# Feed-forward: the gated chunk computed twice from the PSUM bank, once rounded and once in full, in place of a rounding copy

## What is computed

```python
h = silu(x @ w1.T * w1_s) * (x @ w2.T * w2_s)     # 128 -> 512
h = gelu(h @ h1.T * h1_s)                          # 512 -> 512
h = gelu(h @ h2.T * h2_s)                          # 512 -> 512
return h @ w3.T * w3_s                             # 512 -> 128
```

## Time and profile before

| | us |
|---|---|
| median of 3 runs | 766.37 |
| lowest and highest run | 765.67, 766.99 |
| the profiled execution's own time | 768.21 |
| span of the profiled execution | 766.4 |
| TensorE (PE) matmuls busy in the span | 685.7 (89%) |
| VectorE (DVE) busy | 484.8 (63%) |
| ScalarE (ACT) busy | 454.9 (59%) |
| GpSimd (POOL) busy | 431.0 (56%) |
| mean granted TensorE clock | 0.977 of full speed |

### The profile page before, as it was taken

One profiled execution on the slowest core, in us unless ns is written; L12 is line 12 of the kernel. 1 busy time (PEld: TensorE's weight loads), 2 busy tenths in 40 slices (PEclk: granted clock), 3 DMA queues, 4 the chain that ended last, 5 costly groups with the idle time before them and its releaser, 6 DMA issues.

```text
span 766.4 us, 13977 instructions
## 1 busy us (share of the span) xinstructions
PE 685.7 (89%) x4706; PEld 472.0 (62%) x4706; DVE 484.8 (63%) x957; ACT 454.9 (59%) x801; POOL 431.0 (56%) x444
## 2 busy tenths in 40 slices
PE   3789896799999999999999999999878899999996
PEld 1455555477787777665555555555445777777784
DVE  6668885567555586456767767766658356675510
ACT  2677774555665565445656566666665555556663
POOL 4455441377867776433444544543555677777763
PEclk9999998899999999999999999999999999999998
DMA  6110320000000003531645654645111000000000
GB/s 182 39 38 20 62 27 2 0 1 1 0 1 0 0 0 99 177 111 43 209 147 177 239 169 156 229 140 180 57 63 41 16 15 15 14 0 15 15 15 27
DMA packets 33028, 52.47 MB, mean 68 GB/s; under 512 B 4560, under 2 KB 9680, under 8 KB 32976
## 3 DMA queue, kind: packets, MB, share of 16 engines
q1 hardware_dynamic: 32784, 51.53, 21.3%
q10 hardware_dynamic: 192, 0.26, 0.1%
HBM read 27.15 MB, written 24.38 MB: 67 GB/s over the span
## 4 chain that ended last, share of the span: by engine, by line
PE 48%; DVE 13%; POOL 13%; issue 12%; ACT 8%; DMA 5%; ACTq 1%; POOLq 1%; DVEq 0%; SPq 0%
PE banks L220 44%; POOL f_h_lo L1122 5%; POOL f_g_lo L1129 5%; ACT b_prob L1448 2%; DMA b_o_dram<-b_o 2%; DVE xn L182 2%; DVE a_mx L645 2%; PE banks L212 2%; ACT a_prob L548 1%; DMA b_den<-b_o_dram 1%; DVE a_prob L657 1%; DVE f_hidden L1072 1%; DVE a_straight L630 1%; PE banks L957 1%; DVE f_gate L1068 1%
## 5 line engine op out<-in xcount | busy, mean ns | idle before, releaser
L1129 POOL TENSOR_TENSOR f_g_lo<-f_gelu,f_g_hi 128x512 fp32r<-128x512 f32 x128 | 167.9, 1316 | 68.8 <-ACT f_g_hi L1024 68.5
L1023 ACT ACTIVATE f_gelu<-banks,cols 128x512 f32<-128x512 f32 x128 | 88.2, 689 | 141.9 <-PE banks L220 139.3
L220 PE MATMUL banks<-f_g_hi,whi 128*128 128x512 f32 x320 | 132.7, 415 | 15.1 <-POOL f_g_lo L1129 15.1
L1534 DVE TENSOR_REDUCE b_segment_max<-banks 128x6 f32<-128x768 f32 x128 | 116.2, 949 | 45.0 <-PE banks L220 44.6
L1644 POOL TENSOR_SCALAR_AFFINE_SELECT b_prob<-b_prob 128x512 f32<-128x512 f32 x128 | 81.7, 641 | 111.6 <-ACT b_prob L1448 111.4
L1448 ACT ACTIVATE b_prob<-banks 128x768 f32<-128x768 f32 x128 | 102.6, 809 | 63.4 <-PE banks L220 55.0
L220 PE MATMUL banks<-f_g_lo,whi 128*128 128x512 f32 x320 | 128.1, 400 | 0.0
L1122 POOL TENSOR_TENSOR f_h_lo<-f_hidden,f_h_hi 128x512 fp32r<-128x512 f32 x60 | 77.5, 1292 | 58.7 <-DVE f_h_hi L1075 58.7
L220 PE MATMUL banks<-f_h_hi,whi 128*128 128x512 f32 x256 | 104.4, 408 | 3.2 <-POOL f_h_lo L1122 2.7
L220 PE MATMUL banks<-f_h_lo,whi 128*128 128x512 f32 x256 | 102.1, 399 | 0.0
L1024 ACT ACTIVATE f_g_hi<-banks,cols 128x512 fp32r<-128x512 f32 x128 | 87.1, 680 | 0.0
(11 more groups left out here) (124 smaller groups left out, 1052.1 us busy)
## 6 DMA issues: line engine op xcount, KB each, us to landing
f_h_hi<-b_q_dram SPq DMA_DIRECT2D x16, 512.0 KB, 4.0
f_h_lo<-b_k_dram SPq DMA_DIRECT2D x16, 512.0 KB, 5.0
b_o_dram<-b_o SPq DMA_DIRECT2D x8, 1024.0 KB, 4.3
b_q_dram<-b_q_hi SPq DMA_DIRECT2D x16, 256.0 KB, 3.2
b_k_dram<-b_k_hi SPq DMA_DIRECT2D x16, 256.0 KB, 3.3
w_stage<-in_wF SPq DMA_DIRECT2D x8, 352.0 KB, 3.2
b_q_dram<-b_q_lo SPq DMA_DIRECT2D x8, 256.0 KB, 3.4
b_k_dram<-b_k_lo SPq DMA_DIRECT2D x8, 256.0 KB, 3.8
```

The source lines that it names most:

```text
L220: return nc.tensor.matmul(out, lhsT, rhs, start=start, stop=stop)
L1023: nc.scalar.activation(gf[c % 2][:, :], z_bank[c % 2], ACT.Gelu, scale=scale).then_inc(s_gf, 1)
L1129: nc.gpsimd.tensor_tensor(lo[:, c, :], gf[c % 2][:, :], hi[:, c, :].bitcast(F32), ALU.subtract).then_inc(s_glo[c % 2], 1)
L1534: nc.vector.reduce_max(seg[:, g, s, 2 * p:2 * p + 2, :], first_pass[:, 2 * p:2 * p + 2, 0:3 * P].rearrange("p b (c k) -> p b c k", c=3), A ...
```

## The change

In `dve_gate` the copy L1075 goes. In its place the instruction of L1072 is made twice: first with `f_h_hi` as its output, so that the rounding happens at its write, then with `f_hidden` as before. The wait for the buffer of `f_hidden` now stands between the two. Each subtraction waits for both. The order of the rest is unchanged.

```diff
                 dve.wait_ge(s_u, KC * t + c + 1)
+                nc.vector.scalar_tensor_tensor(out=hhi[n.odd][:, c, :], in0=b[:, :], scalar=sc[:, 1, c:c + 1],
+                                               in1=uu[slot][:, :], op0=ALU.mult, op1=ALU.mult).then_inc(s_hhi, 1)
                 dve.wait_ge(s_hlo[slot], 2 * t + c // 2)
                 nc.vector.scalar_tensor_tensor(out=hf[slot][:, :], in0=b[:, :], scalar=sc[:, 1, c:c + 1],
                                                in1=uu[slot][:, :], op0=ALU.mult, op1=ALU.mult).then_inc(s_hf[slot], 1)
-                dve.wait_ge(s_hf[slot], 2 * t + c // 2 + 1)
-                nc.vector.tensor_copy(hhi[n.odd][:, c, :], hf[slot][:, :]).then_inc(s_hhi, 1)
 
             def dve_hlo(dve, n, c):
                 dve.wait_ge(s_hhi, KC * n.t + c + 1)
+                dve.wait_ge(s_hf[c % 2], 2 * n.t + c // 2 + 1)
                 nc.vector.tensor_tensor(hlo[n.odd][:, c, :], hf[c % 2][:, :], hhi[n.odd][:, c, :].bitcast(F32),
                                         ALU.subtract).then_inc(s_hlo[c % 2], 1)
...
             def pool_hlo(pool, n, c):
                 pool.wait_ge(s_hhi, KC * n.t + c + 1)
+                pool.wait_ge(s_hf[c % 2], 2 * n.t + c // 2 + 1)
                 nc.gpsimd.tensor_tensor(hlo[n.odd][:, c, :], hf[c % 2][:, :], hhi[n.odd][:, c, :].bitcast(F32),
                                         ALU.subtract).then_inc(s_hlo[c % 2], 1)
```

## The result

The changed kernel takes 760.35 us in the median of four runs (760.00 to 763.38), the kernel before 766.43 beside it; the ratio is 0.993, with a 95% interval from 0.9903 to 0.9957. A second set of six runs gave 761.15 us against 767.21, ratio 0.9908 (0.9874 to 0.9943).

A forecast was written before the change was run, and what follows sets the result against it. The prediction took a feed-forward block's length to be set by the loop through gate products, VectorE's gate work and copy, and POOL's subtractions, for which TensorE waits. Its terms summed to -2.6 us, giving 763.8 us, range 761.8 to 766.7.

The forecast's parts named there:

- seams of feed-forward 1: Later VectorE work with nothing to hide it: +0.55 us in the head, +0.4 in block 6 of feed-forward 1.
- block 5: In both feed-forwards, POOL's idle times behind the hindered copies go: -0.6 us, of which -0.4 stays in feed-forward 1.
- block 0 of feed-forward 2: Copies of 1.52 and 1.49 us go; with VectorE's later work, the block ends 0.4 us sooner.
- steady block: Eight feed-forward blocks: start 0.21 us later, two POOL subtractions regain 0.27 and 0.18; -0.24 each, -1.9 in all.
- later start: In a steady block, POOL's `f_h_lo` begins 0.21 us later, since the second bank instruction ends after the copy did.
- slower rival: POOL's subtractions stay stretched by other VectorE work, so steady blocks only lose 0.21 us each: +2.9, 769.2 us; chance 0.12.
- no-difference rival: Steady blocks gain half, seams cost their upper bounds: -0.7 us, 765.7 us; chance 0.2.
- much faster one: TensorE's waits for `f_g_lo` vanish wholly in steady blocks and both block 5: -8 us, 758 us; chance 0.06.
- last block of attention B: POOL's masks freed from the copy, -0.26 and some -0.1 us, against +0.21 for VectorE's later `f_h_lo`: net -0.15.

The follow-up runs named there:

- e9: Kernel before, with the second bank instruction only in the four gate chunks of block 0 of feed-forward 2; 764.48 us, ratio 0.9968.
- e7: Changed kernel plus one float32 VectorE copy from SBUF to SBUF, result unused, at the end of each gate chunk; 772.38 us.
- e3: Changed kernel, with the old copy kept in the gates of blocks 0 and 7 of feed-forward 1; 760.22 us, ratio 0.9904.
- e14: Changed kernel, unchanged, profiled again to count falls of the clock; span of 759.3 us in that profile.
- e11: Kernel before, unchanged, profiled again to count falls of the clock; 21.0 us from first to fourth gate in the head of feed-forward 2.
- e5: Kernel before, with the second bank instruction in feed-forward 1 alone, the copy kept in feed-forward 2; 765.95 us, ratio 0.9978.
- e12: Changed kernel, unchanged, profiled again to count falls of the clock; 17.2 us from first to fourth gate in the head of feed-forward 2.

## Why the prediction was wrong

**The steps that were right.** The walk through the seams of feed-forward 1 (+0.55 and +0.4, measured +0.57 and +0.40), block 5 (-0.6, measured -0.56 and -0.57), block 0 of feed-forward 2 (-0.4, measured -0.50). The mechanism of a steady block is as put: later start, POOL's instructions back at 1.29, TensorE's wait shorter. Its size was -0.24 and is -0.31. The later start is +0.10 us there and not +0.21 (`f_h_lo` begins 2.21 us behind the first `f_gate` of the block, 2.11 before; in the head of feed-forward 1 it is 2.27 and 2.01). Two small things make that: behind the first `f_gate` of a block stood 0.13 us of idle time ahead of `f_hidden`, which is 0.03 with the new order, and the second bank instruction takes 0.743 and not 0.751. So 8 x 0.07 = 0.6 us were missed there. (The run of POOL's work in that block has eight instructions, not seven; nothing in the sum hangs on it.) The slower rival is refuted by `f_g_lo` (no instance above 1.36), the no-difference rival by the same rows. The much faster one had 758 us, nearer to the measured 760.35 than the forecast is, but that is luck: it named a wrong place, for TensorE's waits for `f_g_lo` didn't vanish, they shrank by 0.3.

**The step that failed** is the last block of attention B, the term of -0.15. It erred twice. First, in its own terms: I put down one mask of POOL's as freed, -0.26, and some -0.1 for another. The copy met a mask in each of three chunks, and TensorE waited for each; the distance from the first to the fourth gate, without falls, shrank by 0.8 us. Second, and larger: the sum took the clock as the profile before had it, and put a change of it at nothing without a reason. In that profile the fall at 571 us stood in the very stretch that the term was made from, and I read the masks' waits and not the clock beside them. With the copies the clock fell 13 times in 7 profiles there, without them 5 times in 9; at 1.4 us each in the mean that is (1.86 - 0.56) x 1.4 = 1.8 us. Together with the 0.8 that is 2.6 us, beside the 2.8 that e9 measured (its interval: 1.2 to 3.7). Why the copies bring the falls isn't shown; what the rows show is that TensorE waits 0.62 us for the masks beside the copies and 0.35 without the copies. The spare copies of e7 begin when the second mask of the pair is nearly done, and not just ahead of it: the masks keep their 0.63, and the clock didn't fall between these gates. That speaks for the coincidence with the mask as the cost, and not the copy as such, though it is one profile.

**The sum.** From the experiments: feed-forward 1 -1.8 (forecast -0.5; the fall at 346 us can be the difference, which isn't shown, and the interval reaches past zero), the head of feed-forward 2 -2.8 (forecast -0.15), the rest of feed-forward 2 -2.4 (forecast -2.0, with its block 0). That is -7.0, against -6.1 in the first set and -6.1 to -7.1 in the second (medians, ratio); each of the three has an interval of 1.3 to 2 us to either side, so the sum fits but proves little. The range should have been wider downwards: it had no case in which the change alters the clock.

## What to carry to other kernels

A VectorE copy from SBUF to SBUF can be the dearer choice beside a busy POOL, even where it is the shorter instruction (0.43 against 0.74 us): look at the maximum of its duration, and at which POOL instructions are longer than their median while it runs. Where TensorE's clock falls in the stretch that a change touches, treat each fall as a term of its own: count falls over several executions before and after, since one profile shows one draw. And where a reordered pair serves some places and costs in others, choose the form by place: with the short copy kept in the gates of blocks 0 and 7 of feed-forward 1, where nothing covers VectorE's time, e3 was ahead by 1.06 us in the profiles, which the runs' medians (760.22 against 761.15) neither confirm nor refute.

## What the runs showed of the hardware that was not expected

- The same work between the same instructions took 15.6 us at a granted clock of 1.00 (e14) and 21.0 at 0.76 (e11), in a stretch where the two kernels differ only in three copies of 0.43 us against three bank instructions of 0.74.
- Executions of one kernel spread: the kernel before over 8 us in one set (764.5 to 772.7) and 4.6 in another, the changed one over 1 us in a set of six and 3.4 in one of four. That the copies in the head of feed-forward 2 widen the spread isn't shown: e5 with them has 8.6 us, but e9 without them has 4.4 beside 4.6 for the kernel before.
- The mean granted clock of an execution says little of its time: 764.51 us at 0.977 and 769.93 at 0.979 for the same kernel. What a fall costs depends on its place. In the changed kernel's first profile the last 9.9 us are at the lower level, where TensorE is busy 4.87 of 9.90 us. From its last gelu to the end that execution took 11.9 us, another of the same kernel (e12) 9.8 with 1.2 us at the lower level: 2.1 us for 8.7, where a fall of 3.4 us in the head of feed-forward 2 cost 1.0 to 1.5.
- Two bank instructions without dependence overlap by 0.08 us in all 64 chunks, and the second is 0.008 us shorter (0.743 against 0.751).
